# Flamingo block: products with V in four groups of four heads instead of two pairs of groups

## The reference

```python
q = einsum('nle,fe->nlf', Q, Wq); k = ...; v = ...          # 16 heads of 16
p = softmax(where(mask, einsum('nhqd,nhkd->nhqk', q, k) / 4, -inf))
out = einsum('nhqk,nhkd->nhqd', p, v)
x = x + tanh(g_xattn) * (einsum('nle,fe->nlf', out, Wo) + bo)
xq = fake_quant(layernorm(x)); gate = xq @ qWg.T; up = xq @ qWu.T
x = x + tanh(g_ffn) * (fake_quant(silu(gate) * up) @ qWd.T)
```

## Time and profile before

| | us |
|---|---|
| median of 3 runs | 252.2 |
| lowest, highest | 252.03, 253.04 |
| the profiled execution, its own time | 253.46 |
| span of that execution, first to last instruction | 251.8 |
| TensorE busy | 213.9 (85%) |
| VectorE busy | 210.2 (83%) |
| ScalarE busy | 159.9 (64%) |
| GpSimd busy | 137.6 (55%) |
| mean granted TensorE clock, as a share of full speed | 0.958 |

### The profile page before, as it was taken

One profiled execution on the slowest core, in us unless ns is written; L12 is line 12 of the kernel. 1 busy time (PEld: TensorE's weight loads), 2 busy tenths in 40 slices (PEclk: granted clock), 3 DMA queues, 4 the chain that ended last, 5 costly groups with the idle time before them and its releaser, 6 DMA issues.

```text
span 251.8 us, 5441 instructions
## 1 busy us (share of the span) xinstructions
PE 213.9 (85%) x1712; PEld 146.5 (58%) x1712; DVE 210.2 (83%) x419; ACT 159.9 (64%) x293; POOL 137.6 (55%) x241
## 2 busy tenths in 40 slices
PE   6699979979989999999999999989882998944960
PEld 6578878858746666666666666555351544313840
DVE  3378888979898998989999898967967789997991
ACT  2265387476687766677787666767655688856910
POOL 7546557643352544486575938479735533440690
PEclk9999999999999999999999999999798699995996
DMA  6979889999447552555544334000000500000396
GB/s 222 277 205 306 270 266 231 262 241 250 140 132 171 122 130 93 120 126 127 129 112 113 89 95 104 1 1 4 0 4 18 191 0 1 3 1 0 39 133 168
DMA packets 34186, 30.82 MB, mean 122 GB/s; under 512 B 5232, under 2 KB 27760, under 8 KB 34160
## 3 DMA queue, kind: packets, MB, share of 16 engines
q1 hardware_dynamic: 29776, 27.74, 40.5%
q0 software_dynamic: 1360, 1.31, 4.3%
q10 hardware_dynamic: 3024, 1.44, 2.2%
HBM read 20.65 MB, written 9.70 MB: 121 GB/s over the span
## 4 chain that ended last, share of the span: by engine, by line
PE 44%; DVE 19%; ACT 11%; issue 10%; POOL 7%; DMA 4%; SPq 3%; ACTq 0%; POOLq 0%; DVEq 0%
PE bank_o L1448 11%; PE bank_a L1431 8%; PE bank_a L1327 6%; PE bank_b L1417 5%; PE bank_a L1457 4%; ACT arena L765 4%; DMA qk_parts<-arena 3%; DVE h_max L1202 3%; DVE big L1211 2%; DVE arena L1239 2%; PE bank_o L1338 2%; DVE v_all L1245 2%; ACT big L765 2%; POOL big L487 1%; PE bank_a L1300 1%
## 5 line engine op out<-in xcount | busy, mean ns | idle before, releaser
L914 DVE TENSOR_REDUCE neg_max<-bank_b 128x2 f32<-128x512 f32 x128 | 80.3, 672 | 5.2 <-PE bank_b L1316 3.0
L1431 PE MATMUL bank_a<-big 98*128 98x256 bf16 x256 | 49.3, 276 | 5.6 <-ACT arena L765 2.3
L765 ACT ACTIVATE arena<-bank_a 128x512 f32<-128x512 f32 x64 | 34.3, 605 | 14.2 <-PE bank_a L1431 14.2
L1417 PE MATMUL bank_b<-big 96*128 96x256 bf16 x224 | 42.7, 272 | 0.3 <-issue 0.2
L765 ACT ACTIVATE big<-bank_a 128x512 f32<-128x512 f32 x64 | 33.9, 595 | 12.4 <-PE bank_a L1431 12.1
L1431 PEld LDWEIGHTS bank_a<-big 98*128 98x128 bf16 x256 | 20.2, 97 | 24.9 <-issue 9.0
L1327 PE MATMUL bank_a<-arena,w_t 128*128 128x256 f32 x128 | 30.2, 381 | 2.0 <-DVE resid L919 1.5
L1327 PEld LDWEIGHTS bank_a<-arena,w_t 128*128 128x128 f32 x128 | 23.2, 190 | 5.4 <-issue 2.7
L511 POOL TENSOR_TENSOR arena<-resid,arena 128x512 bf16<-128x512 f32 x16 | 18.3, 1157 | 11.1 <-ACT arena L703 11.1
L1417 PEld LDWEIGHTS bank_b<-big 96*128 96x128 bf16 x224 | 21.1, 97 | 4.5 <-issue 0.8
L852 ACT ACTIVATE arena<-bank_b,w_scale_x 128x512 f32<-128x512 f32 (+1 forms) x24 | 16.1, 685 | 5.6 <-DVE big L1211 1.7
(11 more groups left out here) (181 smaller groups left out, 439.3 us busy)
## 6 DMA issues: line engine op xcount, KB each, us to landing
qk_parts<-arena SPq DMA_DIRECT2D x8, 768.0 KB, 5.1
big<-qk_parts SPq DMA_DIRECT2D x32, 192.0 KB, 3.3
big<-qk_parts SPq DMA_DIRECT2D x32, 128.0 KB, 3.3
x_rows<-in_x SPq DMA_DIRECT2D x8, 256.0 KB, 5.2
big<-qk_parts SPq DMA_DIRECT2D x32, 64.0 KB, 3.5
big<-in_ctx SPq DMA_DIRECT2D x7, 256.0 KB, 5.1
out<-x_rows SPq DMA_DIRECT2D x7, 256.0 KB, 3.0
out<-v_all POOLq DMA_DIRECT2D x5, 256.0 KB, 7.5
```

Source lines behind the costliest of these rows:

```text
L765: act.activation(probabilities(h), ring_bank(b, ("exp", h)).rearrange("p (c s) -> p c s", c=QC), ACT.Exp, scale=SCALE).then_inc(exp_done, 1)
L914: dve.tensor_reduce(neg_max[:, p, :, h], bank.rearrange("p (c s) -> p c s", c=QC), axis=AX.X, op=ALU.max, negate=True).then_inc(max_done, 1)
L1417: done = mm(to, q_st[0:KR, p, h, c * P:(c + 1) * P], k_st[0:KR, p, h], start=True, stop=not masked)
L1431: done = mm(to, k_st[0:KM, p, h, k * P:(k + 1) * P], q_st[0:KM, p, h], start=True, stop=not masked)
```

## The change

The table of TensorE's places has four entries for the products with V instead of two. Groups 0, 1 and 2 stand at heads 6, 10 and 14 of their own step, and group 3 at head 2 of the next. Before, groups 0 and 1 stood at head 9 and groups 2 and 3 at head 1 of the next step. The output halves move from heads 11 and 3 to heads 12 and 4, with their evictions on ScalarE, and so the ring of banks has its output places one exponential later. In the last step group 1 moves from head 9 to 10, and the group 2 that stood there by a line of its own is in the table. The lists of VectorE, GpSimd and SP stay as they are.

```diff
-    PE_AT = {"max_tr": 1, ("pv", 1): H + 1, ("out", 1): 2 * H + 3, "next_max_tr": 9, ("pv", 0): 9,
-             ("out", 0): H + 11}
+    PE_AT = {"max_tr": 1, ("pv", 3): H + 2, ("out", 1): 2 * H + 4, ("pv", 0): 6, "next_max_tr": 9, ("pv", 1): 10,
+             ("out", 0): H + 12, ("pv", 2): 14}
...
-    ACT_AT = {"max": 1, ("scaled", 1): 2 * H + 3, "next_max": 9, ("scaled", 0): H + 11}
-
-    PE_LAST = {"max_tr": 1, ("pv", 1): H + 1, ("out", 1): 2 * H + 2, ("out", 0): H + 6, ("out", 2): H + 7, ("pv", 0): 9}
+    ACT_AT = {"max": 1, ("scaled", 1): 2 * H + 4, "next_max": 9, ("scaled", 0): H + 12}
+
+    PE_LAST = {"max_tr": 1, ("pv", 3): H + 1, ("out", 1): 2 * H + 2, ("out", 0): H + 6, ("out", 2): H + 7, ("pv", 0): 9, ("pv", 1): 10, ("pv", 2): H - 2}
...
                     else:
-                        for g in range(2 * what[1], 2 * what[1] + 2):
-                            product_with_v(of, q, g, known == 0 and g == 0)
+                        product_with_v(of, q, what[1], known == 0 and what[1] == 0)
...
-                        if not ahead and h == H - 2:
-                            product_with_v(b, p, 2)
```

## The result

| | before | changed |
|---|---|---|
| median, us | 252.12 | 250.68 |
| lowest to highest of the runs | 251.68 to 253.04 | 250.01 to 251.14 |
| ratio of the times, 95% interval | | 0.9932, 0.9904 to 0.9960 |
| the profiled execution, own time / span | 253.46 / 251.8 | 250.77 / 249.2 |
| step, between output products of head 11 or 12 | 14.16, 14.14; last two 14.53, 14.56 | 13.86, 13.87; last two 14.11, 14.11 |

The change gains 1.4 us by the medians where 3.4 were forecast. The sign and the range hold (250.7 lies in 247.2 to 251.2); the size is off by more than half.

A forecast was written before the change was run, and what follows sets the result against it. TensorE was taken as critical, waiting 1.0 us a step on ScalarE. A stretch of 87.97 us was to become 83.5 of work plus 1.1 of waiting, 84.6, saving 3.4: 248.8 us, range 247.2 to 251.2.

The forecast's parts named there:

- (a): TensorE in a step: two pairs becoming four lone groups add 0.48 us of work; bounds nothing and 0.65.
- (b): TensorE's waits on ScalarE's exponentials: of 1.0 us a step 0.15 stays, 0.25 with the long rounding; three near ties.
- (c): VectorE's turn 1 of the results: waits 0.3 to 0.5 us without backlog, none if one maximum behind.
- Rival 2: VectorE takes over as the bound: steps of 13.9 to 14.0 us, time 250.6 us; chance 0.10.
- (d): Output products and evictions one head later: cost nothing in steps, put 0.44 us on the path to the end.
- (e): Maxima's round trip from an output product's end to head 8's exponential score: 8.1 us within 9.2, hidden, 1 us spare.
- (f): Step 0: group 0 ahead of head 8's exponential score costs 1.10 us in a 1.08 us wait, free within 0.1.
- (g): Last step, from step 6's output product to the first weight transposition: 15 us unchanged, shifts worth -0.5 to +0.5.
- Rival 1: TensorE empties fully at each switch between products and scores: 1.1 us less saved, 249.9 us; chance 0.13.
- Rival 3: VectorE, fully caught up, waits a group's whole 1.10 plus 0.2 us at its turn: 1.8 lost, 254.0 us; chance 0.07.
- Rival 4: TensorE's low clock at the end also covers three more microseconds of matmuls: 3 us come back, 251.8 us; chance 0.10.
- The signs that it named: Steps 13.7 to 13.9 us, TensorE's wait under 0.2, ScalarE's four idle pieces below 0.8; against: 0.3 us idle before exponential scores.

The follow-up runs named there:

- e1: Kernel before, each pair of groups split with one head between the halves (groups at heads 9, 10, 1, 2), outputs unmoved: 255.45 us, ratio 1.012.
- E8: Not a run: TensorE's score pair for the exponential of head 8, here in step 0; starts at 74.99 us before, 74.78 in the changed kernel.
- e4: Changed kernel with ScalarE's weight rounding at head 2 of a step instead of head 3: 249.19 us, ratio 0.987.
- e3: Changed kernel with the output products and their evictions back at heads 11 and 3: 248.36 us, ratio 0.986.
- e12: Kernel before with the rounding at head 1 and the ring's empty place moved behind the transposition of maxima at head 9: 246.37 us, ratio 0.978.
- e2: Kernel before with only the output products and their evictions one head later (heads 12 and 4): 250.55 us, ratio 0.994.
- e7: Kernel before with output products at heads 13 and 5 and the rounding at head 1: 250.78 us, ratio 0.995.
- e6: Kernel before with output products at heads 12 and 4 and the rounding at head 1: 249.22 us, ratio 0.988.
- e10: Kernel before with the rounding at head 1 and only the first output product moved, to head 12: 248.95 us, ratio 0.986.

## Why the prediction came out as it did

- **(a) The split, 0.48 a step: right.** e1 measured 0.49.
- **(b) ScalarE's waits: the mechanism right, the size wrong, and this is the main miss.** The term of the sum that was mis-sized is the waiting, 6 x 0.15 + 2 x 0.1 = 1.1 us, where 3.0 were left (86.48 us from E8 to the output product of step 6, less the 83.5 of work). The shortfall of 1.9 in this stretch is all here. In the five steps from the output product of step 1 on, 0.95 was put in (0.15 in an ordinary step, 0.25 in a long one), and the trace shows 0.25 and 0.49 over the unbroken 13.62, 1.7 in all. For the stretch ahead of them, from E8 to the output product of step 1, that leaves 0.15 of the forecast. It has 15.4 us of work (21 heads, 3 transpositions, 5 groups) and took 16.66: 1.26 of waiting. In these first steps some output products don't exist yet. An E behind such a place waits for the exponential two heads before it, as in every step, but without the 0.87 of an output product in between: the E of head 13 in step 0 and of heads 5 and 6 in step 1 lose 0.19, 0.19 and 0.52. The 0.52 needs the rounding too: with the rounding at head 2 (e4) it is 0.04, and with the missing output's place one head earlier (e3), where by the list the E of head 6 asks for an older bank, it is nothing. No run tested the two waits of 0.19. Two of the three ties that were named turned into waits (exponential 15 before the E of head 1, 0.19 a step; exponential 4 before that of head 6, 0.24 and 0.52), where the forecast gave all of them 0.15 together.
- **(c) VectorE's turn, a wait of 0.3 to 0.5: about right.** It is 0.54, and nothing waits for it: from 105 to 119 us every M starts 0.22 to 0.23 behind its E. Rival 2 gave 250.6, the time measured, but by another cause than the one found: with TensorE's waits gone (e12) VectorE kept up with steps of 13.29. A time that fits a rival does not confirm it.
- **(d) Output products later, nothing in a step, 0.44 at the end: wrong in the step.** In the kernel before, the same move is worth 0.56 a step (e2). It takes the rounding out from behind the eviction, and 0.49 of the 0.56 are that. The reason given, that ScalarE is between exponentials there, left out what else stands in its list. In the changed kernel the move was worth nothing in ordinary steps, as forecast, but with the rounding at head 3 it cost 0.20 in each of two steps and 0.52 in step 1 (e3 against the changed kernel). The 0.44 at the end was right, and is why e3 beats the change.
- **(e) The round trip hidden: right**, and e7 shows that its spare was real and under one more head.
- **(f) Group 0 of step 0 free: right.** E8 started at 74.78, not later than 74.99.
- **(g) 15 us behind the last output product: right**, 14.78.
- **Rival 1** (full emptying) falls by e1. **Rival 3** (the turn makes it slower) falls: the turn waits 0.54, not 1.3. **Rival 4** did not occur in the changed kernel's execution; it was the kernel before whose profiled execution had paid 0.68 for a clock of 0.50 in the last attention stage (14.49 against 13.81, above).
- **The signs that it named:** ordinary steps of 13.87 and 0.19 of waiting before an E lie within them; the long steps do not. ScalarE idles in four pieces of 0.75 to 0.88, not below 0.8; the idle piece of 0.36 in step 1 is the sign by which (b) was to be called wrong. That the time still fell into the range is owed to its width: the saving was well under half of the forecast.

What the prediction did not ask is whether the wait had a cheaper cure. It took 1.0 us of waiting as what the split removes. It had the rounding in view (a part of the 1.0 us, and the whole of the earlier trace rows) and ScalarE's idle time beside the pairs (1.49 us, 1.78 beside the other), and did not put the one into the other.

## What to carry over

Before paying for finer interleaving, list what stands on the waiting engine between its idle time and the wait, and move the work that has no due time into the idle time: here one 0.6 us activation, moved by two heads, gave more than splitting the matmul groups did. Changes that cure the same backlog don't add; try each alone. In a ring of buffers, look at what a padding place or a wrap does to the distance of its neighbours, and put it behind the longest pause of the engine that frees the buffers.

## What the runs showed of the hardware

- A group of eight float32 products with V costs 0.12 us more alone than in a pair (0.49 for four in a step, e1). Part of it is on entry, 0.09 after an M, which a pair pays once for two groups.
- Waits of 0.19 and 0.24 us on TensorE (at 123.09 and 141.60 in the changed kernel) left no idle row, since records of 0.38 at a pace of 0.22 overlap by 0.16; only the spacing of starts shows them.
- TensorE's granted clock fell to half, for 3 to 7 us, in the ten us behind the first weight transposition in some of the profiled executions and not in others. In nine of the fourteen it stayed at 1.00 there, and the stretch from that transposition to the maximum over all rows took 13.80 or 13.81 us in each, whatever the schedule; in before, e1, e6, e7 and e10 it fell, and the stretch took 14.31 to 15.52 (15.45 in e10). A stretch of e10 with nothing but that:

```profile
182.00:184.00 2.00, 2.00 (x6) 1.60 (x5) 0.05 (x1) 0.00 (x0) 0.00 (x0) 0.50 0.00 0
```

TensorE had its full clock (1.00) from 172 to 180, while it transposed weights with gaps between, and had 0.50 in this one. What makes it fall in one execution and not in another stays open; at 0.5 to 1.7 us it is as large as the effect of the change, which is why steps at full clock (1.00 in every stretch compared above) were used to tell the kernels apart.
